# A graph kernel whose experts are moved one step ahead of the edge chunks

## What is computed

```
xn = layernorm(x)                                     # x: 6250 nodes x 256
x  = x + gnn(xn, src, dst) + mix(xn)                  # 100000 edges; linear attention
x  = x + ffn(layernorm(x))

def ffn(x):                                           # padded to 49 tiles of 128 nodes
    h = x @ W_gat                                     # 4 heads x 4 experts
    e = leaky_relu(a_src[src] + a_dst[dst], 0.2)      # 131072 edges, sorted by dst in the kernel
    alpha = softmax of e over the edges of each dst
    agg = segment_sum(h[src] * alpha, dst) + b_gat
    scores = layernorm(agg) -> mean over heads -> top 2 of 4 experts -> softmax weights g
    return sum over experts of g * (gelu(x @ W1[e] + b1[e]) @ W2[e] + b2[e])
```

## Time and profile before

| | us |
|---|---|
| median of 3 runs | 2744.48 (2743.87 to 2746.11) |
| the profiled execution's own time | 2745.59 |
| its span, first to last instruction | 2743.2 |
| busy in it: PE / DVE / ACT / POOL | 1507.4 / 2122.8 / 1299.4 / 1918.7 |

### The profile page before, as it was taken

One profiled execution on the slowest core, in us unless ns is written; L12 is line 12 of the kernel. 1 busy time (PEld: TensorE's weight loads), 2 busy tenths in 40 slices (PEclk: granted clock), 3 DMA queues, 4 the chain that ended last, 5 costly groups with the idle time before them and its releaser, 6 DMA issues. The chain is left out here.

```text
span 2743.2 us, 23603 instructions
## 1 busy us (share of the span) xinstructions
PE 1507.4 (55%) x5746; PEld 949.8 (35%) x5746; DVE 2122.8 (77%) x3511; ACT 1299.4 (47%) x3173; POOL 1918.7 (70%) x1938
## 2 busy tenths in 40 slices
PE   5567340123233233232153399999999999996223
PEld 3333140011111111111053166666666666652023
DVE  7988868899999999998493566666666666668567
ACT  4422116899999999998152123222223222320022
POOL 3677686777777777776466877777777777777450
PEclk9878675555555555555555699999999999997566
DMA  7517654777778777775751422222222222222295
GB/s 220 190 43 229 216 172 161 260 249 254 260 239 277 259 254 271 234 256 176 224 168 33 121 53 53 53 53 53 53 53 57 62 60 56 53 60 42 60 313 214
DMA packets 224584, 419.46 MB, mean 153 GB/s; under 512 B 50805, under 2 KB 173586, under 8 KB 217024
## 3 DMA queue, kind: packets, MB, share of 16 engines
q1 hardware_dynamic: 133780, 279.68, 28.9%
q0 software_dynamic: 74512, 123.31, 19.2%
q10 hardware_dynamic: 16156, 14.98, 1.7%
HBM read 217.05 MB, written 200.79 MB: 152 GB/s over the span
## 5 line engine op out<-in xcount | busy, mean ns | idle before, releaser
L1281 POOL DMA_INDIRECT stage_got<-ffn_rows,setup_src_ffn x815 | 808.9, 993 | 248.2 <-issue 248.1
L1281 POOL DMA_INDIRECT edges_got<-gnn_rows,edges_src_gnn x644 | 609.6, 947 | 197.3 <-issue 194.4
L1395 DVE TENSOR_TENSOR_SCAN stage_y<-stage_decays,stage_y 128x960 f32<-128x960 f32 (+2 forms) x256 | 520.8, 2089 | 5.8 <-issue 5.7
L1411 ACT ACTIVATE stage_rows<-stage_y 128x3640 f32<-128x3640 f32 (+1 forms) x88 | 400.5, 4551 | 0.0
L2236 PE MATMUL stage_ph<-ffn_xt_all,stage_w 128*128 128x448 f32 x896 | 366.0, 547 | 60.3 <-ACT stage_hid L2297 29.2
L2366 DVE TENSOR_TENSOR stage_start_parts<-stage_pk,stage_of_tile 128x392 f32<-128x392 f32 x418 | 219.0, 562 | 95.1 <-PE stage_pk L2228 86.9
L2228 PE MATMUL stage_pk<-stage_start_parts 128*128 128x392 bf16 x1236 | 252.0, 342 | 63.1 <-DVE stage_start_parts L2366 51.3
L1701 PE MATMUL stage_pm<-setup_ident,stage_mix_parts 128*128 128x128 f32 x98 | 32.4, 434 | 434.0 <-ACT stage_mix_parts L1724 424.6
L1371 DVE TENSOR_TENSOR stage_y<-edges_got,stage_weights 128x896 f32<-128x896 f32 x168 | 262.5, 1666 | 0.3 <-ACT stage_weights L1350 0.3
L2236 PEld LDWEIGHTS stage_ph<-ffn_xt_all,stage_w 128*128 128x128 f32 x896 | 169.0, 192 | 195.7 <-issue 136.0
L2369 DVE TENSOR_REDUCE stage_got<-stage_start_parts 128x16 f32<-128x784 f32 x209 | 202.8, 970 | 20.1 <-issue 1.3
(11 more groups left out here) (489 smaller groups left out, 3123.8 us busy)
## 6 DMA issues: line engine op xcount, KB each, us to landing
state_gnn<-stage_rows SPq DMA_DIRECT2D x56, 1848.0 KB
y<-search_found SPq DMA_DIRECT2D x28, 896.0 KB, 4.1
tail_fin_y<-y SPq DMA_DIRECT2D x7, 3584.0 KB, 17.3
stage_got<-ffn_rows,setup_src_ffn POOLq DMA_INDIRECT x815
state_ffn<-stage_rows SPq DMA_DIRECT2D x32, 384.0 KB, 2.4
edges_got<-gnn_rows,edges_src_gnn POOLq DMA_INDIRECT x700, 3.5
staged_rows<-rows_staged SPq DMA_DIRECT2D x12, 910.0 KB, 4.8
edges_got<-staged_rows SPq DMA_DIRECT2D x6, 1820.0 KB, 13.8
```

The lines of the kernel that those rows point to most:

```text
L1281: pool.indirect_dma_start(out=got[:, u, t, :], out_offset=None, in_=self.row_dram[g.name][:, :], in_offset=bass.IndirectOffsetOnAxis(ap=sr ...
L1395: ins = dve.tensor_tensor_scan(some, r[s][:, 0:b - a, :].rearrange("p c t -> p (c t)"), some, 0.0, ALU.mult, ALU.add)
L1411: act.activation(rows[:, s, :, 0:C + H], y[:, s, :, 1:T + 1].rearrange("p c t -> p t c"), ACT.Copy).then_inc(rows_ready, 1)
```

## The change

DVE's loop is taken apart into `results(q)` (everything that followed the chunk in a step: takes, picked columns of chunk q+1, sources, choose of chunk q+2) and `chunk(c)`. It now runs `results(0)` first and then, for each c, `chunk(c)` followed by `results(c + 1)`. ACT makes the gelus of steps 0 and 1 before its loop, and the gelus of step q+2 after the factors of chunk q. SP loads lanes and stores in the matching order. After the last step the nine picked columns are those of chunk c+2 rather than c+1. There is one more `drain` between `sources` and `choose`. `PICKED` goes from (7, 6, 7, 6) to (7, 7, 7, 6). PE's and POOL's programs are not edited; their counts follow `PICKED`.

```
-PICKED, PICKED_LATE = (7, 6, 7, 6), 9
+PICKED, PICKED_LATE = (7, 7, 7, 6), 9
...
+                def store_y(q):
+                    sp.wait_ge(out_used, q * BANKS + BANKS)
+                    sp.dma_start(by_tile[:, at(q % blocks * B, B), q // blocks, :], yrow[:, :, :]).then_inc(y_out, 16)
                 load_lanes(1)
-
-                def step(b, e, q, s):
-                    load_lanes(q + 2)
-                    edge.sp_store(sp, q, s)
-                    sp.wait_ge(out_used, q * BANKS + BANKS)
-                    sp.dma_start(by_tile[:, at(b * B, B), e, :], yrow[:, :, :]).then_inc(y_out, 16)
-                walk(step)
-                for c in range(steps, FFN.chunks):
-                    load_lanes(c + 2)
+                load_lanes(2)
+                store_y(0)
+                for c in range(FFN.chunks):
+                    load_lanes(c + 3)
                     edge.sp_store(sp, c, c % 2)
+                    if c + 1 < steps:
+                        store_y(c + 1)
...
                 def step(b, e, q, s):
                     factors(q, s)
-                    if q + 1 < steps:
-                        gelus((q + 1) // blocks, q + 1, 1 - s)
+                    if q + 2 < steps:
+                        gelus((q + 2) // blocks, q + 2, s)
                     edge.act_rows(act, q, q // 2, s, s)
                 edge.act_first(act)
                 gelus(0, 0, 0)
+                gelus(0, 1, 1)
                 walk(step)
...
-                def step(b, e, q, s):
-                    chunk(q, q // 2, s)
+                def results(q):
                     if q > 0:
                         dve.wait_ge(y_out, q * 16)
                     for k in range(BANKS):
-                        take(e, q, k)
+                        take(q // blocks, q, k)
                         for j in of_pair(q + 1, k):
                             take_picked(q + 1, j)
                     dve.drain()
                     sources(q + 1)
+                    dve.drain()
                     choose(q + 2)
-                walk(step)
-                for c in range(steps, FFN.chunks):
+                results(0)
+                for c in range(FFN.chunks):
                     chunk(c, c // 2, c % 2)
-                    if c + 1 < FFN.chunks:
-                        for j in range(picked(FFN, c + 1)):
-                            take_picked(c + 1, j)
+                    if c + 1 < steps:
+                        results(c + 1)
+                    elif c + 2 < FFN.chunks:
+                        for j in range(picked(FFN, c + 2)):
+                            take_picked(c + 2, j)
                         dve.drain()
-                        sources(c + 1)
+                        sources(c + 2)
                         dve.drain()
-                        choose(c + 2)
+                        choose(c + 3)
```

## The result

The changed kernel takes 2782.17 us (median of 4 runs, 2779.28 to 2786.71) where the kernel before, on the same chip, takes 2744.59 (2743.87 to 2746.11). The ratio is 1.014 with a 95% interval of 1.0128 to 1.0152: 37.6 us slower, where 35.8 were forecast. The profiled execution took 2779.28 us, the lowest of the four; its span is 2777.2.

A forecast was written before the change was run, and what follows sets the result against it. Inner steps were taken to run at the pace of the DVE, ACT and PE loop, with POOL slack until the end; columns 14.1, drain 4.8 and tail 16.9 sum to 35.8 us over 2744.5, forecast 2780 us, range 2764 to 2787.

The forecast's parts named there:

- The inner step keeps its order: Inner steps: every engine's order stays, PE still waits for the gelu behind a chunk's exponentials; the move's price there is zero.
- The start: Chunk 0 comes after results(0), at 1610.7; POOL stands still 19 us before chunk 2's gathers, not felt by DVE at once.
- The seventh column: Inner steps: seven chunks go from six picked columns to seven at 2.01 us each, 14.1 us, ends 6.9 and 15.3.
- that PE would set it (6.9): Part of rival "cheap steps" (chance 0.12): a pick costs PE's 0.99 us, so the columns cost 6.9 us; 2768 in all.
- The drain: Between last pick and chunk, on the loop: 0.17 us in each of 28 results, 4.8 us; lower end nothing.
- the rival read from it that an added drain is free: Part of rival "cheap steps" (chance 0.12): the added drain costs nothing, the sum is 4.8 us smaller by that.
- The tail: From the last results to chunk 31: one chunk more and POOL late, 98.9 us against 82.05, 16.9 us later.
- I also expected DVE to wait before chunk 30: Tail: DVE was to stand idle on gathers before chunks 30 and 31, a sign that the forecast is right.

The follow-up runs named there:

- The move without its drain: Changed kernel with the old column counts (7, 6, 7, 6) and without the added drain, so only the chunk's place differs from the kernel before: 2761.75 us, ratio 1.0066.
- a turn of ACT's order: Changed kernel with the first two gelus of the step ahead put before the factors of the chunk, the other two after: 2754.32 us.
- The three slots: Changed kernel with three slots of got instead of two, and one output bias loaded instead of four to make room: 2771.55 us.
- only ACT's order was turned: Kernel before with the first two gelus of the step ahead put before the chunk's factors, the other two after: 2734.86 us, ratio 0.9968.

## Why the prediction was right

**The inner step keeps its order.** Shown. The move without its drain takes 878.35 us for the 27 steps, against 878.64 before. PE's wait for the gelu stayed, and only a turn of ACT's order removed it.

**The start.** Right in place and size: POOL stood 18.24 us (19 forecast), and counted from PE's step 0 chunk 0 started 37.34 us on, where 1610.7 - 1573.38 = 37.3 were forecast. The three slots show that this wait by itself costs nothing.

**The seventh column.** 14.1 forecast, 13.65 measured alone. DVE's price was the nearer end; that PE would set it (6.9) is out. In the traces the six columns of the steps cost somewhat more than 2.01 us each: 14.3 in the order of before, 13.9 in the moved order without the drain. Behind the drain they cost 10.4, so these two terms do not simply add.

**The drain.** The mis-sized term. I priced its gap, 4.8 us; it measured 6.9 in the changed kernel, 7.9 in the one before and 9.7 in the moved order with the old counts. The Trainium skill (VectorE: DVE Perf Modes, "The DRAIN you can't avoid") says that the pipeline is emptied behind every op; the rival read from it that an added drain is free, and every one of the three disagrees with that reading. The section adds that "A next op that is not held starts earlier", and the rows agree with this part: without the drain the gap is -0.08 us. What my term left out is the instructions behind the drain that meet the end of a gather.

**The tail.** 16.9 forecast, 17.6 measured for the move alone. In the changed kernel it was 15.2: POOL began chunk 27 at 57.0 us before the last results' end instead of 55.6, as step 27 took 28.93 us instead of 27.44, and the chain of gathers took 152.8 (153.1 forecast). PE's granted clock was 0.83 in that step (0.92 before), between its levels of 1.2 and 2.4 GHz:

```profile
2478.90:2507.80 28.90, 19.33 (x83) 12.75 (x81) 22.71 (x39) 2.93 (x7) 22.07 (x23) 0.83 0.26 64
```

Early in that step PE works only 1.26 of 4 us in both kernels, and the clock is lower after that: 0.57 and 0.57 in the next two stretches of 4 us, against 0.65 and 0.92 before. The other traces, without the one in which DVE waits for gathers at this step, have 27.9 to 29.4 us at 0.82 to 0.87, so the 27.44 that I took for a fixed length is the shortest of all. Why the clock came back sooner in that one stays open. I also expected DVE to wait before chunk 30; it did not, that chunk's gathers were in 15.4 us ahead.

**The number.** The mechanism was right, and that 35.8 came so near to 37.6 is in part luck. By the traces the start cost 2.2 us, as forecast; the 27 steps cost 20.3 where six columns and 27 drains had been put at 16.7; the tail cost 15.2 where 16.9 had been. Two errors of opposite sign leave 1.9. The parts measured alone, 17.6 for the move, 13.65 for the columns and 7.9 for the drain, sum to 39.2.

## What to carry to other kernels

Moving a job one step ahead frees nothing if every engine keeps the same order relative to the others: write out each engine's sequence with the step numbers shifted, and look whether any wait has changed its partner. A shift can then cost at the ends, in the chunk that is left over and in whatever waits for a buffer that the shifted job frees: here 17.5 us behind the last results, and nothing at the start. To remove a wait, turn the order on the engine that is waited for (here ACT), and then share the time won between the two engines that arrive at the end together.

## What the hardware showed unexpectedly

An engine that shows no wait was still paced by another. POOL's 815 gathers took 1057.0 us in the kernel before and 1047.1 when only ACT's order was turned. All of that lies in the gathers themselves, 808.9 us against 799.0; the pauses are 248.2 in both. A gather takes 0.94 us, but 1.06 to 2.18 when it is the last to meet the scan behind line 1363 (line 1395), as at 1612.88, 1646.69 and 2450.81 above. In the kernel before, DVE's scan of chunk 8 and POOL's two gathers beside it:

```profile
1842.61 1.53 DVE L1395 TENSOR_TENSOR_SCAN stage_y<-stage_decays,stage_y 128x660 f32<-128x660 f32 x1 [0.16 <-issue]
```

```profile
1841.52 1.61 POOL L1281 DMA_INDIRECT stage_got<-ffn_rows,setup_src_ffn  x1 [0.30 <-issue]
1843.44 1.45 POOL L1281 DMA_INDIRECT stage_got<-ffn_rows,setup_src_ffn  x1 [0.30 <-issue]
```

The second gather ends at 1844.89, 0.75 us after the scan. That is no accident of one step: in the twelve traces 371 scans meet a gather, and each time the last gather that meets it ends 0.74 to 0.77 us after the scan's end. So the scan sets POOL's position anew in every chunk, which no row of waits shows. In the kernel before, each chunk's gathers ended the same 11.3 to 13.7 us before DVE's start of it from chunk 1 to chunk 27. That these meetings alone keep the lead so steady is argued, not shown: in the kernel before with the drain they occur as well, and the lead grows from 12.7 to 28.3 us. The meetings act the other way too: a copy of 4 columns on DVE took 0.41 us at the end of a gather instead of 0.16.
